# Window attention and a per-channel blur: a new order of ScalarE's copies, of values and projections, and four constant matmuls in two steps

## The reference, cut to what matters

```
x = x + attention(group_norm(x, 32 groups))   # 7x7 windows, 12 heads of 16 channels
x = x + blur(group_norm(x, 32 groups))

attention: q, k, v = 1x1 products of x with w_qkv
           dots = q.k * scale + bias;  softmax over 49;  out = attn @ v
           return w_proj @ out + b_proj
blur:      each of 8 blocks of 24 channels is shifted by a whole offset, then
           convolved with its own normalised 5x5 Gaussian (depthwise)
```

## Time and profile before

| | |
|---|---|
| median of 3 runs | 6182.63 us |
| profiled execution | 6163.97 us |
| its span | 6162.2 us |
| TensorE busy | 5409.0 us (88%) |
| VectorE, ScalarE, GpSimd busy | 4255.1, 3790.8, 3580.1 us |
| mean granted TensorE clock | 0.929 |

### The profile page before, as it was taken

How to read it: one execution, slowest core, us unless ns; L and a number is a source line. 1 busy time by engine, 2 the same in 40 slices (tenths; PEclk the granted TensorE clock), 3 DMA queues, 4 the chain that set the end, 5 groups by cost and what they waited for, 6 DMA issues and landing times. The chain is left out here.

```text
span 6162.2 us, 258882 instructions
## 1 busy us (share of the span) xinstructions
PE 5409.0 (88%) x97992; PEld 4490.2 (73%) x97992; DVE 4255.1 (69%) x9682; ACT 3790.8 (62%) x8451; POOL 3580.1 (58%) x3940
## 2 busy tenths in 40 slices
PE   5888889988898888889888898888898889899896
PEld 3777777777777777777777777777777777777775
DVE  3776667777777767777767777767777766677763
ACT  1666666666666666666666666666666666666662
POOL 0565556665556655566655566655566655566654
PEclk9999999999999999999999999999999998999996
DMA  2555655555655555655555655555655555555553
GB/s 61 123 130 138 138 134 120 129 134 136 139 134 117 135 135 132 141 132 118 137 134 133 143 127 122 137 133 136 137 128 127 134 137 134 134 123 127 133 118 72
DMA packets 1352972, 790.32 MB, mean 128 GB/s; under 512 B 1187528, under 2 KB 1237128, under 8 KB 1344008
## 3 DMA queue, kind: packets, MB, share of 16 engines
q1 hardware_dynamic: 1351816, 774.03, 55.1%
HBM read 157.09 MB, written 154.14 MB: 51 GB/s over the span
## 5 line engine op out<-in xcount | busy, mean ns | idle before, releaser
L1207 POOL TENSOR_TENSOR o<-osb,o 128x192 f16<-128x192 f32 x1024 | 624.5, 610 | 1768.8 <-ACT o L840 1754.1
L1201 POOL TENSOR_TENSOR probl<-prob,probh 98x588 f16<-98x588 f32 x1024 | 1332.5, 1301 | 298.1 <-DVE probh L1045 183.8
L637 PE MATMUL pO<-vv,probh 98*49 98x34 f16 x24576 | 1023.2, 225 | 103.9 <-ACT om L848 85.6
L637 PEld LDWEIGHTS pO<-vv,probh 98*49 98x49 f16 x24576 | 872.6, 122 | 313.1 <-issue 251.7
L832 ACT ACTIVATE mov<-pT 12x98 f16<-12x98 f32 x1024 | 248.1, 242 | 1329.6 <-PE pT L604 1329.5
L637 PE MATMUL pO<-vv,probl 98*49 98x34 f16 x12288 | 995.2, 228 | 54.5 <-issue 54.5
L637 PEld LDWEIGHTS pO<-vv,probl 98*49 98x49 f16 x12288 | 778.0, 122 | 58.4 <-issue 58.3
L1030 DVE TENSOR_REDUCE mx<-pS 128x12 f32<-128x588 f32 x1024 | 777.2, 759 | 34.1 <-issue 15.9
L620 PE MATMUL pT<-qst,kst 96*98 96x49 f16 x12288 | 760.4, 208 | 11.5 <-issue 11.4
L827 ACT ACTIVATE prob<-pT 98x588 f32<-98x588 f32 x1024 | 672.3, 657 | 105.8 <-PE pT L620 97.2
L620 PEld LDWEIGHTS pT<-qst,kst 96*98 96x98 f16 x12288 | 696.5, 133 | 13.8 <-issue 13.6
(11 more groups left out here) (190 smaller groups left out, 16140.3 us busy)
## 6 DMA issues: line engine op xcount, KB each, us to landing
kst<-kh SPq DMA_DIRECT2D x1536, 98.0 KB, 2.2
qst<-qh SPq DMA_DIRECT2D x1536, 49.0 KB, 2.3
qst<-mix SPq DMA_DIRECT2D x768, 98.0 KB, 2.9
kst<-mix SPq DMA_DIRECT2D x768, 98.0 KB, 2.2
vv<-cv SPq DMA_DIRECT2D x1024, 73.5 KB
xr<-x_scratch SPq DMA_DIRECT2D x32, 2352.0 KB, 12.3
out<-xr SPq DMA_DIRECT2D x256, 294.0 KB
x_scratch<-xm SPq DMA_DIRECT2D x256, 196.0 KB, 3.3
```

Of the source, the lines that this page charges most:

```text
L637: mm = pe.matmul(pO[64 * win:64 * win + NT, OW * hp:OW * hp + OW], b[0:98, p % 2, PW * hp + NT * win:PW * hp + NT * win + NT], vv[:, g % 2 ...
L1201: pool.tensor_tensor(probl[0:98, p % 2, :], prob[0:98, p % 2, :], probh[0:98, p % 2, :], ALU.subtract).then_inc(S["pl_p"], 1)
L1207: pool.tensor_tensor(o16[:, p % 2, C:2 * C], osb[:, p % 2, :], o16[:, p % 2, 0:C], ALU.subtract).then_inc(S["ol_p"], 1)
```

## The change

Projections, the residual, the second statistics, x1's last store and the blur move one step later. The norm moves one step earlier, and on ScalarE its full copy stands ahead of `shift_hi` and its f16 copy behind `turned_out`. Values go to even steps, `LEAD` becomes 6; in a step without a q/k product and without a blur (4 and 12 of the full body) they stand ahead of `turn_out`. In steps 5 and 12 TensorE gets four matmuls of constants whose result nothing reads. x1 is read back in two halves, at steps 6 and 8 of SP. VectorE's first six statistics of the next image go from two steps to three. The diff, cut:

```
-LEAD = 5
+LEAD = 6
+IDLE = (5, 12,)
 def norm_step(p, att, nxt):
-            for lo, shift, c, on in ((2, 0, 2, att), (10, 0, 3, att), (18, 1, 0, nxt), (26, 1, 1, nxt)):
+            for lo, shift, c, on in ((1, 0, 2, att), (9, 0, 3, att), (17, 1, 0, nxt), (25, 1, 1, nxt)):
 def v_step(p, att, nxt):
-            if p % 2 and (att if p + LEAD < PAIRS else nxt):
+            if p % 2 == 0 and (att if p + LEAD < PAIRS else nxt):
 def proj_step(p, prev, att):
-                    s = PPR * r + 6 + (LATE_TAIL if tail and r < NWX - 1 else 0)
+                    s = PPR * r + 7 + (0 if not tail else LATE_TAIL if r < NWX - 1 else 1)
 # SyncE
-            def read_x1():
-                sp.dma_start(xr[0:SY, :], scratch.rearrange("s y c x -> (s y) (c x)")).then_inc(S["xr_in"], 16)
+            def read_x1(s):
+                sp.dma_start(xr[HW * s:HW * s + HW, :],
+                             scratch[s].rearrange("y c x -> y (c x)")).then_inc(S["xr_in"], 16)
-                    v = before(v_step, p, prev, att, nxt) if p % PPR == 2 else None
+                    v = before(v_step, p, prev, att, nxt) if p % PPR == 1 else None
-                    if p == 5 and prev:
+                    if p == 6 and prev:
...
-                        read_x1()
-                    if p in (2, 6) and nxt:
+                        read_x1(0)
+                    if p == 8 and prev:
+                        read_x1(1)
+                    if p in (2, 7) and nxt:
 # TensorE
+            def keep_busy(i, p):
+                pe.wait_ge(S["qk_dve"], nth("qk_dve", i, 6 * (p // PPC + 1) + 6))
+                for _ in range(4):
+                    pe.matmul(pQ[:, 0:ROW], addb[:, :], biasT[:, 0:ROW], start=True, stop=True,
+                              skip_group_check=True)
+            def given_back(i, was):
+                for n, row, tail in was:
+                    if tail_bank(row if tail else 0) is pV:
+                        pe.wait_ge(S["pj_act"], nth("pj_act", i + n, 2 * row + tail + 1))
                     if q:
                         qk(i + q[0], q[1], q[2])
+                    v = v_step(p, att, nxt)
+                    early = v and not q and b is None
+                    if early:
+                        given_back(i, was)
+                        values(i + v[0], v[1])
+                    if prev and nxt and p in IDLE:
+                        keep_busy(i, p)
...
-                    if v:
+                    if v and not early:
+                        given_back(i, was)
                         values(i + v[0], v[1])
 # ScalarE: norm(i, c, s, hi) makes one copy, xnf (hi False) or xnh / xnt (hi True)
                     for n, row, tail in before(proj_step, p, prev, att, nxt):
                         project_out(i + n, row, tail)
+                    n, q = norm_step(p, att, nxt), qk_step(p, att, nxt)
+                    if n:
+                        norm(i + n[0], n[1], n[2], False)
                     if att:
                         shift_hi(i, p)
...
-                    n = norm_step(p, att, nxt)
-                    if n:
-                        norm(i + n[0], n[1], n[2])
-                    q = qk_step(p, att, nxt)
                     if q:
                         qk_hi(i + q[0], q[1], q[2])
-                    for n, q in at(p, 3, prev, att, nxt):
-                        turned_out(i + n, q)
+                    for m, o in at(p, 3, prev, att, nxt):
+                        turned_out(i + m, o)
+                    if n:
+                        norm(i + n[0], n[1], n[2], True)
 # VectorE
-                    if nxt and p in (6, 7, 10, 11):
+                    if nxt and p in (6, 7, 8, 10, 11):
-                        first = {6: 0, 7: 3, 10: 6, 11: 9}[p]
-                        for r in range(first, first + 3):
+                        first, n = {6: (0, 2), 7: (2, 2), 8: (4, 2), 10: (6, 3), 11: (9, 3)}[p]
+                        for r in range(first, first + n):
```

More of the change, by code:

```diff
@@ L730, in body @@
                         group_sum(1, pQ, gmv[0][:, :, 0] if p == 12 else gv[0]).then_inc(S["gn1_pe"], 1)
-                    if prev and p == 5:
+                    if prev and p == 6:
                         pe.wait_ge(S["pj_act"], nth("pj_act", i - 1, 16))
@@ L758, in _, with norm @@
             act.wait_ge(S["setup"], SET_ALL)
-            def norm(i, c, s):
+            def norm(i, c, s, hi):
                 row, tail = 2 * c + s % 2, s // 2
[L763 to L774, removed]
+                if not hi:
+                    act.wait_ge(S["gn1_pool"], nth("gn1_pool", i, 2))
+                    done = PPC // 2 * (c - 1) - (0 if s % 2 else 2)
+                    if due("v_pe", i, done):
+                        act.wait_ge(S["v_pe"], nth("v_pe", i, done))
+                    if due("qk_pe", i, 6 * (c - 1)):
+                        act.wait_ge(S["qk_pe"], nth("qk_pe", i, 6 * (c - 1)))
+                    if tail:
+                        act.wait_ge(S["xnl_p"], nth("xnl_p", i, 2 * c + s - 1))
+                    elif due("xtl_d", i, 2 * c + s - 1):
+                        act.wait_ge(S["xtl_d"], nth("xtl_d", i, 2 * c + s - 1))
                 t = slice(ROW * (row % 4), ROW * (row % 4) + ROW)
@@ L778, in norm @@
                     src, g = windows(xt[h:h + 64, par(i), u]), slice(h, h + 64)
-                    hi, full = xnt[0:64, t], xnf[0:64, s % 2, :]
+                    o = xnt[0:64, t] if hi else xnf[0:64, s % 2, :]
                 else:
                     src, g = windows(xm[:, par(i), ROW * row:ROW * row + ROW]), slice(0, 128)
[L782 to L786, removed]
+                    o = xnh[:, t] if hi else xnf[:, s % 2, :]
+                a = act.activation(wmajor(o), src, ACT.Identity, bias=gbias[g, tail:tail + 1],
+                                   scale=grs[0][g, tail:tail + 1])
+                if hi:
+                    a.then_inc(S["xnh_a"], 1)
             def qk_hi(i, c, g):
@@ L1120, in body @@
                         tail_lo(i + m[0], m[1], m[2])
-                    if prev and p == 10:
+                    if prev and p == 11:
                         dve.wait_ge(S["gn2_pe"], nth("gn2_pe", i - 1, 3))
@@ L1126, in body @@
                         v_lo(i + v[0], v[1])
-                    if prev and p == 7:
+                    if prev and p == 8:
                         add_eps(1, i - 1, pM)
-                    b = blur_step(p, 13, prev)
+                    b = blur_step(p, 14, prev)
                     if b is not None:
@@ L1134, in body @@
                                                  op1=ALU.subtract).then_inc(S["z_dve"], 1)
-                    if prev and p == 6:
+                    if prev and p == 7:
                         center(1, i - 1, pM)
@@ L1140, in body @@
                                      ).then_inc(S["gn2_bn"], 1)
-                    for n, t, on in ((0, 0, att and p == 26), (0, 1, att and p == 30), (-1, 2, prev and p == 2),
-                                     (-1, 3, prev and p == 4)):
+                    for n, t, on in ((0, 0, att and p == 27), (0, 1, att and p == 31), (-1, 2, prev and p == 3),
+                                     (-1, 3, prev and p == 5)):
                         if on:
@@ L1156, in body @@
                             dve.bn_stats(gst[0][:, r, :], src).then_inc(S["gn1_bn"], 1)
-                    if prev and p == 8:
+                    if prev and p == 9:
                         dve.wait_ge(S["gn2_pool"], nth("gn2_pool", i - 1, 1))
```

30 lines of the change are left out of this document (15 added, 15 removed).

## The result

The changed kernel takes 5952.74 us (median of 4 runs, 5932.22 to 5960.88), the kernel before 6182.55 in runs beside it. The ratio is 0.9628, its 95% interval 0.9596 to 0.9661: 3.7% faster. Forecast were 5690 us and a range of 5500 to 5910. The direction was right, the size was not: the gain is 230 us where about 490 were forecast. The profiled execution has a span of 5945.8 us, 216.4 less than before.

A forecast was written before the change was run, and what follows sets the result against it. The prediction took TensorE's own work, its waits (om, xnt and others) and its low clock to bound the kernel. Its terms summed to -480 us, 6164 to 5684, about 5690 with the medians' offset; range 5500 to 5910.

The forecast's parts named there:

- Projections -190: Projections one step later on TensorE: nearly all of their 194.4 us wait for om goes, -190 us.
- xnt -140: Norm one step earlier: the q/k products' 146.3 us wait for xnt on TensorE goes, -140 us.
- attention for om -60: ScalarE's f16 norm copy behind om: attention's 85.6 us wait for om loses most, -60 us.
- New order on ScalarE +75: Full norm copy ahead of mov on ScalarE delays the shifted scores: 2.4 us a body, +75 us.
- Values early -15: Value matmuls early in steps 4 and 12 fill TensorE's idle time for osb and mov: -15 us net.
- The step that failed: Costs of GpSimd's tighter norm steps and SP's some 200 issues in a shrinking body: +40 us, bounds 0 and 150.
- The clock -185: Three quarters of the 245 us lost to TensorE's low clock come back as waits leave: -185 us, bounds 0 and 245.
- the 28% of the prediction: Share of TensorE's low-clock time taken as lost, from step 5 of images 20 and 21: 245 of 875 us.
- The read in halves -25: x1 read in halves, values spread before it: a third of TensorE's 56.7 + 15.9 us waits goes, -25 us.
- The clock still falls: Rival, chance 0.18: waits go, but steps 4 to 6 stay thin and 875 us stay at low clock; 5869 us.
- ScalarE and GpSimd take TensorE's place: Rival, chance 0.14: full copy delays shifted scores 0.65 us in 16 norm steps, 322 us for 75; 5931 us.
- The slower rival: Chance 0.04: read's second half lands near step 12, GpSimd and TensorE stand in step 11, clock falls; 6240 us.

The follow-up runs named there:

- experiment 16: Changed kernel with x1 read in four pieces, values never early, next image's first load earlier, six k copies on ScalarE's queue two at a time: 5632.05 us, 0.9119.
- experiment 3: Changed kernel with x1 read back for only 8 of 96 channels: 5738.57 us, 0.9264 of the kernel before.
- experiment 9: Changed kernel without the spreading of values and with x1 read for only 8 of 96 channels: 5612.23 us, 0.9096 of the kernel before.
- experiment 12: Changed kernel with values behind the shifted scores in all steps, never early in steps 4 and 12: 5910.62 us, 0.9577 of the kernel before.
- experiments 13 and 14: Kernel before, without the spreading of values (13: ratio 0.9922) or with x1 read for only 8 of 96 channels (14: ratio 0.9838).
- experiment 5: Changed kernel with x1 read back whole, in one transfer at step 6: 5950.90 us, 0.9619 of the kernel before.
- experiment 7: Changed kernel with x1 read in four pieces by channels at steps 6, 8, 10 and 12, each waited for separately: 5826.25 us, 0.9428.
- experiment 6: Changed kernel with the second half of x1's read issued ahead of the 12 stack copies of step 8: 5966.07 us, 0.9654.
- experiment 10: Changed kernel with x1 read in four pieces and six k copies in one block on ScalarE's queue, ending steps 5 and 13: 5777.88 us, 0.9362.
- experiment 11: Changed kernel with x1 read in four pieces, six k copies in one ScalarE block, next image's first load ahead of step 2's k copies: 5782.64 us, 0.9369.

## Why the prediction was wrong

*Projections -190, xnt -140, attention for om -60:* right as to the waits (0.9, 9.8 and 1.2 us are left). Step 16 kept 5.28 and step 18 fell from 7.05 to 5.28, as forecast.

*New order on ScalarE +75:* too dear. Shifted scores wait 16.5 us for mov in all. What shows instead is VectorE in the blur's steps: its z and its sum into xr make the first product wait 83.4 and 67.8 us, so steps 19, 21 and 27 take 6.31, 5.79 and 6.18 us. Experiment 16 has the same two. Before they were 44.0 and 10.4, so 97 more: not in the sum. The scores' wait for mx, 0.7 before and 46.5 now, is not in it either; 30.5 of it stay in experiments 3 and 9, so most of it is not due to late transfers. Together these waits for VectorE have grown by 143 us, where the sum had 75 for a wait that did not come. Which edit brings them no run tells.

*Constants +20, first statistics 0:* within what can be measured. *Values early -15:* wrong sign (experiment 12: the time falls by 32 us without them).

*The step that failed* is the one on queues: "SP takes 7.96 us to issue 12 stack copies and has some 200 issues (counted in the code) in a body that shrinks. For these two +40, bounds 0 and 150." Together with the read's -25 it priced transfers near nothing. From the traces: TensorE's waits for transfers or without a releaser are 201 us in all (77.7 for kst, the rest without a releaser) against 101 before (17.3, 68.3 and 15.9 for vv), so 100 more, where the two terms made +15 together. By the runs: with both causes out the changed kernel gains 329 us, and the kernel before about 148 if experiments 13 and 14 add (the pair was not run). So some 180 us of the cost are new, low clock included. I had the parts in hand, the count and 7.96/12 = 0.66 us a copy, and did not multiply: 200 issues at that rate are 132 us of a body. The trace of before has 167 of 186.2, and they are spread evenly over the body. The clock's term hung on this one, as shown below.

*The account by waits.* Gone: 414 us (-390 forecast). Transfers and no releaser: +100 (+15). VectorE (z, xr, mx): +143 (+75, priced at another wait). osb and mov: -26 (-15). Clock: -32 (-185), as worked out below. That makes -229, and the span fell by 216. So the three terms that failed are the clock by 153, the transfers by 85 and the waits at VectorE by 68.

*The clock -185:* wrong as a size, and as a cause. I gave it to TensorE's gaps for `om` and to thin steps, and counted on the constants. Low time fell from 875 to 2 x 0.064 x 5946 = 761 us, an eighth instead of three quarters; at the 28% of the prediction that is 32 us and not 185. The gaps in steps 6, 9 and 11 stand beside transfers that are late or in a burst, and the low clock behind them. Where these are in order and values late, it comes as forecast: in experiment 16 it is 2 x 0.020 x 5625 = 225 us, three quarters less than before. With the transfers' causes out and values early it is 2 x 0.041 x 5610 = 460 us (experiment 9). So the clock's term hung on the queue's term and, besides, on the place of the values. The 28% comes from one pair of steps and was not tested.

*The read in halves -25:* nothing (experiment 5). The idle time without a releaser grew from 56.7 us at L637 to 90.4 and 30.3 at other lines. The Trainium skill (Runtime: NRT & Kernel Launch, Instruction fetch mechanics) says that instruction fetch hides behind issue; by that rule a lighter burst could free nothing. The traces do not agree: each long stand ends 1.26 to 1.78 us behind the end of an instruction packet, experiment 3 has none of them left, and experiment 7 cuts the largest wait to 34.0. So beside a burst the fetch is most likely not hidden. No run moved the fetch by itself.

*The rivals.* "The clock still falls" (5869) came nearest in its mechanism and was 84 us under the median, having no price for SyncE. "ScalarE and GpSimd take TensorE's place" (5931) came nearest in time, and by another way: its sign, a wait for mov over 100 us, did not come. The slower rival named the place rightly, GpSimd waiting for xr in each body (106.1 us, 31 times), but experiment 6 shows that this wait alone costs nothing.

Open: why the instruction packets come too late beside the read, since a packet itself takes no longer in the changed kernel than before (1.8 us at most in both); what brings the low clock to step 13 where values are early; how much of the waits at VectorE can be had back; and whether GpSimd's queue would carry the copies as well as ScalarE's (not tried).

## What to carry to other kernels

An engine that only issues transfers has a busy time too. Before shortening steps, add up its issues stretch by stretch (83 of 89.5 us here) and set them against the shorter stretch; if little is left, move issues or drop some first. The sum does not say which stretch will lose: look there for the copies that are wanted at once and for large transfers. A large transfer in a short body is a burst with a price on other engines: cut it in pieces spread over steps, and check by leaving most of its bytes out. A low clock is a sign and not a term: look for the gap ahead of it, and where there is none, try another order of TensorE's own work. Where TensorE stands for nothing in straight code, look for an instruction packet in the DMA queues.

## What the runs showed of the hardware that was not expected

- An issue's time on SyncE hardly depends on its bytes: 12 copies of 49 KB (qst<-qh) take 9.83 us and 12 of 98 KB (kst<-kh) 9.66; four spreads with an eighth of the rows 3.0 against 3.38. Behind the read the same four take 11.96 us, and 3.37 when that is small (experiment 3).
- Issues on ScalarE hold that engine up as well: six in a block made TensorE wait 64.5 us for `prob` (experiment 10). Two at a time that wait is off the list (experiment 16). Late values came in between, so the 155 us from experiment 11 to 16 are not the block's alone.
- Four pieces of the same read cost 2% less than two, and two the same as one.
- TensorE's stands of over 1 us without a releaser, 201 in seven traces, all end 1.26 to 1.78 us behind the end of a 16 KB instruction packet. All but three stand within 14 us behind the issue of a read of x1, and they are gone when it is cut to 8 of 96 channels (experiments 3 and 9).
